# Query, key and value projections as plain f32 products in an attention and routed feed-forward kernel

## What is computed

```python
style = cond @ affine_w.T + affine_b                 # modulated linear layer
y = clip(modulated_linear(x, style), -256, 256)
q = layernorm(y) * norm_g + norm_b  @ Wq             # 16 heads of 64: 1024 columns
k, v = y @ Wk, y @ Wv                                # 1024 columns each
q, k = l2norm(q) * q_scale, l2norm(k) * k_scale
x1 = x + softmax(q @ k.T + alibi, with 2 null keys) @ v @ Wout
...
```

## Time and profile before

| | |
|---|---|
| median of 3 runs | 2233.7 us (2231.6 to 2236.91) |
| the profiled execution, own time | 2237.69 us |
| its span, first to last instruction | 2235.9 us |
| mean granted TensorE clock | 0.959 of full speed |
| TensorE busy with matmuls | 1914.6 us |
| VectorE busy | 1747.7 us |
| ScalarE busy | 1334.1 us |
| GpSimd busy | 729.9 us |

### The profile page before, as it was taken

How to read it: one execution, slowest core, us unless ns; L and a number is a source line. 1 busy time by engine, 2 the same in 40 slices (tenths; PEclk the granted TensorE clock), 3 DMA queues, 4 the chain that set the end, 5 groups by cost and what they waited for, 6 DMA issues and landing times.

```text
span 2235.9 us, 64818 instructions
## 1 busy us (share of the span) xinstructions
PE 1914.6 (86%) x25286; PEld 1508.1 (67%) x25286; DVE 1747.7 (78%) x4574; ACT 1334.1 (60%) x2769; POOL 729.9 (33%) x647
## 2 busy tenths in 40 slices
PE   4789888889898888988888888888888988899863
PEld 3577776767776676777767677667776766677652
DVE  5567888888878888888888888887888888888644
ACT  3456666665666666566566656666665665666441
POOL 0332333333333333333333333333334333333211
PEclk8889999999999999999999999999999999999865
DMA  3011111111111111111111111111111111111110
GB/s 130 6 25 37 39 35 37 41 34 36 36 36 36 35 40 31 38 38 40 32 35 41 31 38 38 37 36 33 42 31 38 38 35 36 36 41 27 37 37 22
DMA packets 337973, 83.11 MB, mean 37 GB/s; under 512 B 277006, under 2 KB 336878, under 8 KB 337902
## 3 DMA queue, kind: packets, MB, share of 16 engines
q1 hardware_dynamic: 337902, 82.12, 16.4%
HBM read 48.51 MB, written 33.55 MB: 37 GB/s over the span
## 4 chain that ended last, share of the span: by engine, by line
DVE 49%; PE 28%; ACT 16%; issue 5%; POOL 1%; ACTq 0%; DVEq 0%; DMA 0%; SPq 0%; POOLq 0%
PE pa L446 11%; DVE pr L1111 7%; DVE nrm L1028 6%; ACT bd L808 4%; DVE mx L1086 4%; DVE pr L1088 4%; DVE qn L1037 3%; PE pc L646 3%; DVE den L1107 3%; DVE pr L1081 3%; PE pa L453 3%; ACT kcat L722 3%; DVE y L1067 2%; ACT L821 2%; ACT qp L727 2%
## 5 line engine op out<-in xcount | busy, mean ns | idle before, releaser
L1173 POOL TENSOR_TENSOR rn<-nrg,mhalf 128x16 f32<-128x16 f32 x128 | 372.2, 2908 | 620.9 <-DVE nrg L1031 620.9
L1028 DVE TENSOR_REDUCE nrm<-sq 128x16 f32<-128x1024 f32 x128 | 155.6, 1216 | 250.9 <-ACT qn L712 250.9
L1178 POOL TENSOR_TENSOR yn<-yn,gb 128x256 f32<-128x256 f32 x64 | 47.1, 736 | 734.4 <-DVE yn L1004 734.4
L711 ACT ACTIVATE sq<-pa 128x512 f32<-128x512 f32 x256 | 152.1, 594 | 192.6 <-PE pa L446 187.3
L484 PE MATMUL ps<-wout,qp 128*128 128x256 f32 x1024 | 245.6, 383 | 0.0
L446 PE MATMUL pa<-wv,y 128*128 128x512 f32 x768 | 217.9, 421 | 0.6 <-DVE pr L1083 0.6
L446 PE MATMUL pa<-wk,y 128*128 128x512 f32 x768 | 215.9, 417 | 0.0
L446 PE MATMUL pa<-wq,xnTs 128*128 128x512 f32 x768 | 213.2, 415 | 2.0 <-DVE xnTs L1134 1.8
L484 PEld LDWEIGHTS ps<-wout,qp 128*128 128x128 f32 x1024 | 190.1, 191 | 27.0 <-issue 0.3
L1111 DVE TENSOR_TENSOR pr<-pr,rden 128x1056 f32<-128x1056 f32 x64 | 171.1, 2674 | 2.2
L446 PEld LDWEIGHTS pa<-wv,y 128*128 128x128 f32 x768 | 138.8, 194 | 35.2 <-issue 10.1
(11 more groups left out here) (214 smaller groups left out, 4811.0 us busy)
## 6 DMA issues: line engine op xcount, KB each, us to landing
xT<-in_xT SPq DMA_DIRECT2D x64, 128.0 KB, 2.1
x<-in_x SPq DMA_DIRECT2D x64, 128.0 KB, 2.7
x1d<-x SPq DMA_DIRECT2D x64, 128.0 KB, 1.7
kxdr<-kxn SPq DMA_DIRECT2D x64, 128.0 KB, 1.7
vm<-kxdr SPq DMA_DIRECT2D x128, 64.0 KB, 2.8
odr<-o SPq DMA_DIRECT2D x256, 32.0 KB, 1.9
on<-odr SPq DMA_DIRECT2D x64, 128.0 KB, 2.0
xb<-x1d SPq DMA_DIRECT2D x64, 128.0 KB, 2.3
```

Of the source, the lines that this page charges most:

```text
L711: fn(sq[:, cols_], pa[:, h, :], ACT.Square)
L1028: v.tensor_reduce(nrm[:, n, :], sq[:, :].rearrange("p (h d) -> p h d", d=DH), AX, ALU.add)\
L1173: g.tensor_tensor(rn[:, n, :], nrg[:, n, :], mhalf[:, :], ALU.pow)\
```

## The change

A half becomes two plain f32 products, one for each chunk. The tiles `wq`, `wk`, `wv`, `y3` hold one f32 value in place of two parts, `xnTs` and `wvraw` are gone, and `xnT` has two buffers. The six operations ahead of the steps that split the weights are gone, and in each step L795 and L1134 (queries) and L1064, L1067 and L1069 (keys and values). `y_nat` is transposed from `y3`, and its semaphore `yT_done` is now raised by the second write of `y3`. TensorE waits for `xnT_done` where it waited for `xnT_parts`.

```diff
-        wq = sb("wq", [P, 2, CK, INNER])
+        wq = sb("wq", [P, CK, INNER])
...
-        xnT = sb("xnT", [P, CK, P])
-        xnTs = sb("xnTs", [P, 2, 2, CK, P])
+        xnT = sb("xnT", [P, 2, CK, P])
...
-            ld("wk_in", raw_w["wk"], in_chunks("Wk"))
+            ld("wk_in", wk[:, :, :], in_chunks("Wk"))
...
             def project(bank, lhs, rhs):
-                n = 0
                 for k in range(CK):
-                    for a_, b_ in ((0, 0), (0, 1), (1, 0)):
-                        last = mm(bank, part(lhs(a_, k)), part(rhs(b_, k)), start=(n == 0), stop=(n == 3 * CK - 1))
-                        n += 1
+                    last = mm(bank, lhs(k), rhs(k), start=(k == 0), stop=(k == CK - 1))
                 return last
...
-                    wait(pe, "xnT_parts", t1)
+                    wait(pe, "xnT_done", t1)
...
-            for w, n in ((wk, "wk"), (wv, "wv"), (wq, "wq")):
-                loaded(act, n + "_in")
-                fn(part(w[:, 0, :, :]), raw_w[n], ACT.Copy).then_inc(S("high_parts"), 1)
...
-                        last = fn(xnT[:, k, :], pa[:, 2, k * P:(k + 1) * P], ACT.Identity,
+                        last = fn(xnT[:, p, k, :], pa[:, 2, k * P:(k + 1) * P], ACT.Identity,
                                   bias=cols[:, NBI, k:k + 1], scale=cols[:, NG, k:k + 1])
                     last.then_inc(S("xnT_done"), 1)
-                    wait(act, "xnT_done", i)
-                    fn(part(xnTs[:, p, 0, :, :]), xnT[:, :, :], ACT.Copy).then_inc(S("xnT_high"), 1)
...
-            for n, (w, name) in enumerate(((wk, "wk"), (wv, "wv"), (wq, "wq"))):
-                dve.wait_ge(S("high_parts"), n + 1)
-                ins = v.tensor_tensor(part(w[:, 1, :, :]), raw_w[name], w[:, 0, :, :], ALU.subtract)
-                ins.then_inc(S("low_parts"), 1)
-            dve.wait_ge(S("low_parts"), 3)
...
-                    v.tensor_scalar(part(y3[:, p, 0, :, 0:BT, :]), yT[:, :, :, :], -CLAMP, None, ALU.max)
-                    v.tensor_scalar(part(y3[:, p, 0, :, BT, :]), yT[:, :, 0, :], -CLAMP, None, ALU.max)\
-                        .then_inc(S("y_high"), 1)
-                    wait(dve, "y_high", i)
-                    v.tensor_scalar(yT[:, :, :, :], yT[:, :, :, :], -CLAMP, None, ALU.max)\
+                    v.tensor_scalar(y3[:, p, :, 0:BT, :], yT[:, :, :, :], -CLAMP, None, ALU.max)
+                    v.tensor_scalar(y3[:, p, :, BT, :], yT[:, :, 0, :], -CLAMP, None, ALU.max)\
                         .then_inc(S("yT_done"), 1)
-                    wait(dve, "yT_done", i)
-                    v.tensor_tensor(part(y3[:, p, 1, :, 0:BT, :]), yT[:, :, :, :], y3[:, p, 0, :, 0:BT, :],
-                                    ALU.subtract)
-                    v.tensor_tensor(part(y3[:, p, 1, :, BT, :]), yT[:, :, 0, :], y3[:, p, 0, :, BT, :],
-                                    ALU.subtract).then_inc(S("yT_low"), 1)
...
-                    wait(dve, "xnT_high", i)
-                    v.tensor_tensor(part(xnTs[:, p, 1, :, :]), xnT[:, :, :], xnTs[:, p, 0, :, :], ALU.subtract)\
-                        .then_inc(S("xnT_parts"), 1)
```

More of the change, by code:

```diff
@@ L96, in adaln_attention_ffn @@
         wo2 = sb("wo2", [P, CK, C])
-        wq = sb("wq", [P, 2, CK, INNER])
-        wk = sb("wk", [P, 2, CK, INNER])
-        wv = sb("wv", [P, 2, CK, INNER])
+        wq = sb("wq", [P, CK, INNER])
+        wk = sb("wk", [P, CK, INNER])
+        wv = sb("wv", [P, CK, INNER])
         wout = sb("wout", [P, HP, C])
@@ L125, in adaln_attention_ffn @@
         vcat = sb("vcat", [P, 2, HP, 2, DH])
-        wvraw = sb("wvraw", [P, CK, INNER])
         pr = sb("pr", [P, HP, 2, J])
-        y3 = sb("y3", [P, 2, 2, CK, BT + 1, L])
+        y3 = sb("y3", [P, 2, CK, BT + 1, L])
         oT = pT
@@ L189, in bc @@
             return u.broadcast_to(shape)
-        def part(ap):
-            return ap.bitcast(mybir.dt.float32r)
         def two(bank, lo):
@@ L203, in adaln_attention_ffn @@
         condT = rawT[:, 3 * C:3 * C + NB]
[L204 to L207, removed]
         chunks = lambda z: z.rearrange("p (k c) -> p k c", k=CK)
@@ L259, in load_all @@
             ld("small_in", wsc[:, :, NS:NS + CH], in_chunks("L0_ffn_compress_w1"))
-            ld("wk_in", raw_w["wk"], in_chunks("Wk"))
-            ld("wv_in", raw_w["wv"], in_chunks("Wv"))
-            ld("wq_in", raw_w["wq"], in_chunks("L0_attn_Wq"))
+            ld("wk_in", wk[:, :, :], in_chunks("Wk"))
+            ld("wv_in", wv[:, :, :], in_chunks("Wv"))
+            ld("wq_in", wq[:, :, :], in_chunks("L0_attn_Wq"))
             ld("late_in", wout[:, :, :], A["L0_attn_Wout"].rearrange("(r p) n -> p r n", p=P))
@@ L417, in _ @@
             pe.wait_ge(S("setup_act"), 1)
+            loaded(pe, "wk_in", "wv_in", "wq_in")
             pe.wait_ge(S("setup_dve"), 1)
@@ L455, in four @@
                 return last
-            yTf = yT[:, :, :, :].rearrange("p k b l -> p k (b l)")
-            y3f = y3[:, :, :, :, :, :].rearrange("p r a k b l -> p r a k (b l)")
-            wv4 = wv[:, :, :, :].rearrange("p a k (r e d) -> p a k r e d", r=HP, e=2)
+            y3f = y3[:, :, :, :, :].rearrange("p r k b l -> p r k (b l)")
+            wv4 = wv[:, :, :].rearrange("p k (r e d) -> p k r e d", r=HP, e=2)
             HEADS = ([(r, t, s) for r in range(R7) for t, s in ((0, 0), (1, 1), (1, 0), (0, 1))]
@@ L468, in q_half @@
                 def q_half(h):
-                    project(pa[:, h, :], lambda a_, k: xnTs[:, 1 - p, a_, k, :],
-                            lambda a_, k: wq[:, a_, k, h * 512:(h + 1) * 512]).then_inc(S("q_mm"), 1)
+                    project(pa[:, h, :], lambda k: xnT[:, 1 - p, k, :],
+                            lambda k: wq[:, k, h * 512:(h + 1) * 512]).then_inc(S("q_mm"), 1)
                 def k_half(h):
                     wait_part(pe, "q_raw", t1, h + 1, 2)
-                    project(pa[:, h, :], lambda a_, k: y3f[:, 1 - p, a_, k, 0:P],
-                            lambda a_, k: wk[:, a_, k, h * 512:(h + 1) * 512]).then_inc(S("k_mm"), 1)
+                    project(pa[:, h, :], lambda k: y3f[:, 1 - p, k, 0:P],
+                            lambda k: wk[:, k, h * 512:(h + 1) * 512]).then_inc(S("k_mm"), 1)
                 def v_half(e):
                     wait_part(pe, "k_raw", t1, e + 1, 2)
-                    project(pa[:, e, :], lambda a_, k: y3f[:, 1 - p, a_, k, e * L:e * L + P],
-                            lambda a_, k: wv4[:, a_, k, :, e, :]).then_inc(S("v_mm"), 1)
+                    project(pa[:, e, :], lambda k: y3f[:, 1 - p, k, e * L:e * L + P],
+                            lambda k: wv4[:, k, :, e, :]).then_inc(S("v_mm"), 1)
                 def out_half(r0):
@@ L583, in step @@
                     wait(pe, "yT_done", i)
-                    from_T(two(pa[:, 2, :], C), yTf).then_inc(S("y_nat"), 1)
+                    from_T(two(pa[:, 2, :], C), y3f[:, p, :, 0:P]).then_inc(S("y_nat"), 1)
                 if live(i, 5):
@@ L1131, in step @@
                     gates()
-                if live(i, 0):
-                    wait(dve, "xnT_high", i)
-                    v.tensor_tensor(part(xnTs[:, p, 1, :, :]), xnT[:, :, :], xnTs[:, p, 0, :, :], ALU.subtract)\
-                        .then_inc(S("xnT_parts"), 1)
                 if live(i, 3):
```

## The result

The changed kernel takes 2265.8 us (median of 4 runs, 2265.1 to 2268.4) where the kernel before takes 2233.2 us on the same chip (4 runs, 2231.6 to 2236.9). The ratio is 1.0146, with a 95% interval of 1.0131 to 1.0160: 33 us slower. The forecast was 2227 us and the range ended at 2254, so the prediction was wrong, 39 us too low.

A forecast was written before the change was run, and what follows sets the result against it. It took a step as a ring of VectorE, TensorE and ScalarE, none full. Start 0.0, steps 9 to 64 -4.5, clock falls -2 sum to -6.5 us: 2233.7 - 6.5 = 2227 us, range 2218 to 2254.

The forecast's parts named there:

- A half, d: One projection half (such as q1, k0 or v1) on TensorE; d is how much longer it gets, 0.32 us.
- The far bound: Highest cost of a projection half: an f32 record of 0.466 us, so the half gets 0.47 us longer.
- that way to the slower side: Rival: TensorE takes more time than VectorE gives; 2263 us, chance 0.22.
- Leg 1: Step from q1's start to VectorE's first score operation; TensorE would set it instead of VectorE, 0.40 us shorter.
- The waits of leg 2: TensorE's waits ahead of `zT` and `xn`: 1.64 us down to 0.28, and 0.72 down to 0.40.
- Leg 2: Step from VectorE's first score operation to v1; claimed unchanged, if TensorE is in time.
- Leg 3: Step from v1 to the next q1; v1 is on it, so 0.32 us longer.
- -4.5: Sum over steps 9 to 64, -0.08 us a step in 56 steps.
- Ahead of step 9: Work ahead of the steps and steps 0 to 8: 9.9 us saved and 9.9 us added, sum 0.0.
- Clock falls: 7 us stretches at half clock, one behind the `kxn` wait; four before, two taken after, 3.0 us each: -2 us.
- the room: Time the scores are ready before VectorE takes them, beyond the shortest hand-over: 1.04 us, gone after the change.
- four would be +4, none -8: Clock-fall cases: all four stay, +4 us (rival, 2233 us, chance 0.17), or none stays, -8 us.

The follow-up runs named there:

- e1: Changed kernel with two idle f32 products (512 and 256 columns) ahead of TensorE's wait for `kxn` in every second step; 2223.6 us, ratio 0.9952.
- e4: Kernel before with all its splitting into parts kept, but only the high parts multiplied, as plain f32 products; 2303.3 us, ratio 1.0314.
- e3: Kernel before with six float32r products a half kept, but the tokens not split in the steps (low parts missing from the sum); 2219.5 us, ratio 0.9936.
- e2: Kernel before with two idle f32 products (512 and 256 columns) ahead of TensorE's wait for `kxn` in every second step; 2232.1 us, ratio 0.9995.
- e7: Kernel before with q1 moved ahead of TensorE's wait for `kxn`; 2209.5 us, ratio 0.9899.
- e9b: Kernel before with q1 moved ahead of the wait for `kxn` and the gather product behind the linear layer; 2217.2 us, ratio 0.9937.
- e5: Changed kernel with one more small ScalarE operation (128x1) ahead of the Gelu, in one step of two; 2281.8 us, ratio 1.0215.
- e6: Changed kernel with q1 moved ahead of TensorE's wait for `kxn`; 2200.2 us, ratio 0.9852.
- e8: Changed kernel with q1 moved ahead of the wait for `kxn` and the gather product behind the linear layer; 2162.9 us, ratio 0.9682.
- e12b: Changed kernel with q1 ahead of the wait for `kxn` and the gather behind the linear layer, repeated on another chip; 2161.0 us, ratio 0.9688.
- e10b: Kernel before with the two idle f32 products ahead of both TensorE waits, for `kxn` and for `zT`; 2223.1 us, ratio 0.9964.

## Why the prediction was wrong, point by point

- **A half, d = 0.32 us: right.** Four f32 records last 1.88 us in a row and one 0.59 (the group of 1018.56 in e1), so they start (1.88 - 0.59)/3 = 0.43 us apart, on the line of the rows of 128 and 256 columns. The far bound, d = 0.47 by passes of equal length, is excluded, and with it that way to the slower side.
- **Leg 1: right.** TensorE sets it, slack 0.05 us, and it is 0.47 shorter (0.40 predicted).
- **The waits of leg 2: right.** `zT` 0.38 us (0.28 predicted), `xn` 0.40 (0.40). Leg 2 is 0.09 longer, which I had at nothing: the first record of v1 starts 0.27 us behind the transposes of `xn` where it was 0.19. This comes with the f32 products and not with the parts, for e4 has it and e3 does not.
- **Leg 3: +0.41 and +0.32**, predicted +0.32. The larger figure is that of the way into a step without the Gelu: there q1 starts 0.12 us later behind the start of q0 than before (1.83 against 1.71), so q0 adds a tenth of a us, which I had at nothing. So a pair of steps went from 65.05 to 65.04 us, where I had -0.16: 28 pairs make this -0.3 us and not -4.5.
- **Ahead of step 9:** predicted 0.0, measured -3.9 us at q1 of step 8 in the two profiled executions. Most of that is chance. Four traces have the code of the kernel before up to this step (before, e2, e7, e9b) and reach q0 of step 8 at 236.4 to 238.4 us; six have that of the changed kernel (after, e1, e5, e6, e8, e12b) and reach it at 234.5 to 237.9. The means are 237.5 and 236.3: -1.1 us, within the spread that the clock of the first steps makes. The prediction put the clock of the first and the last steps at nothing, and between two single executions it is worth several us.
- **Clock falls: the step that failed.** "I take two: 6 - 8 = -2 us". The mechanism and the price of one were right: it lies behind the wait for `kxn`, and with the room gone it costs 3.1 us (3.0 predicted; leg 1 of 11.99 against 8.90) where it cost 2.0. The number was 15, which lay outside "four would be +4, none -8": 15 x 3.1 - 4 x 2.0 = +38 us. The text said that steps of another length can bring more, and then gave that no case and no chance; it even took "TensorE idles less" as a reason for fewer. Only its last line named many falls as a sign of being wrong.

What speaks for a cause of the number: in the kernel before the four falls are 457.4 us apart each time, seven pairs of 65.05 and the 2.0 of a fall; after the change 133.1 and 68.3 us are two pairs or one, and the 3.1 of a fall (2 x 65.04 + 3.09 = 133.2). These sums hold for any falls that stand behind the same wait; what says more is how they drift. The falls at 506, 639, 772, 905 and 1038 begin 1.22, 1.19, 1.14, 1.11 and 1.07 us behind the start of q1, and the next one, at 1106, begins at 1.22 again. So the falls begin at times that drift against the step, which fits a beat between the steps and whatever decides on the clock. The pair kept its length to 0.01 us, the shift by each fall did not, and e5 has more falls with a pair that is 0.07 us longer. That the wait is needed is shown (e1, e6, e8: no falls; e10b: none once both waits are filled); that the larger shift brings the next wait sooner to the unlucky place fits the spacings, but was only argued. The wait itself changed too, from 1.96 to some 1.6 us, and no run keeps that apart. So the cause of the number stays open. The count itself I could not have derived, and cannot now: e3, e4, e7 and e9b have 21 to 27 falls.

## What to carry to other kernels

Work taken from the engine that sets a leg is worth at most the room up to the next engine, here 1.0 of 1.29 us, and what the next engine gets in exchange comes off that: read both ways to the hand-over before the change is costed, and look again once the order is another (the same exchange was worth about 1 us here, would cost some 12 in the order of e6, and gave 26 in that of e8). The room also hid a third of each clock fall, so where the trace of a periodic kernel shows even a few falls behind a wait, "the falls multiply" is a case of its own in the sum: here 3.1 us in every pair of steps or every second. The cure cost nothing here: put independent work into the wait, real work first (e8, 2163 us), idle products where there is none (e1, 2224).

## What the runs showed that I had not expected

- Idle times of TensorE of 1.0 us in all, in two pieces (0.58 and 0.50, e7), stand right ahead of a fall; single ones of 1.4 to 2.0 us do in the other places. Filling one wait of two moved the falls to the other (e2) and left the time as it was.
- A fall is not of one length. In the changed kernel all are 6.8 us at the lower level and cost 3.1 us; behind the wait for `zT` in e2 they are 3.4 us and cost 1.2. Behind the wait for `kxn` both lengths occur (e3: eleven of 6.8 and twelve of 3.4 us).
- More TensorE work made the kernel faster: e1 executes 24634 matmul records where the changed kernel executes 24518, and is 42 us shorter.
